# Graph network block: the first dense product starts per block of the counts' matrix; key comparison in loops from broadcast rows

## The chip, the cores and the metric

One core of a Trainium2 chip runs the whole program. The metric is the time of one execution in microseconds (us), the median of three runs. The core has TensorE (PE, matrix products), VectorE (DVE), ScalarE (ACT), GpSimd (POOL) and SyncE (SP), which run side by side and meet at semaphores. DMA engines move data between the core's memory and the chip's.

## The reference, cut to what matters

Four graph layers follow one another over 6250 nodes with 128 features and 100,000 edges sorted by destination. The part that matters here is the first layer, whose aggregation is applied twice:

```python
N_NODES, N_EDGES, D, K, ALPHA = 6250, 100000, 128, 2, 0.5
dst = jnp.minimum((6250 * uniform(100000) ** 2.0).astype(int32), 99999)   # sorted: low nodes hold most edges
for _ in range(K):
    msg = norm[:, None] * x[src]
    agg = jax.ops.segment_sum(msg, dst, num_segments=n)
    x = (1.0 - ALPHA) * agg + ALPHA * h
```

The second layer (edge attention), the third (two mean aggregations) and the fourth (gated sums) use the same edges. The third applies the same unweighted aggregation twice more.

## The kernel before, in words

**The matrix of counts.** The four unweighted aggregations are done as dense products. A matrix of bf16 counts lies in the chip's memory (`d_adj`): 52 row blocks (`VBLOCKS`) of 128 rows, and 49 column blocks (`BLOCKS`) of 128 source nodes. Its rows are numbered in the order in which destination nodes first appear among the sorted edges, with one extra row at every boundary between pairs of tiles, so edges that come later write rows that lie later.

**How it is filled.** SP first fills it with zeros (`zero_sp`, L455, 52 transfers). The 782 tiles of 128 edges are then written by GpSimd (`scatter_pool`, L474): one indirect DMA for each tile, 128 elements of two bytes each, to the addresses in one column of `address`. At most 16 tiles are under way (`adj_out`). Tiles are grouped in 49 batches of 16 (`BATCH * U`).

**Equal edges.** Two edges of a pair of tiles with the same source and destination must not be written twice: one of them must write the total count and the other must be sent elsewhere. So every batch is compared before it is written. TensorE turns each tile's keys (`key_col`) into rows in PSUM (`same_pe`, L557); VectorE compares a pair's row of 256 keys with the column of one tile (`same_dve`, L569) and sums what is equal, which leaves a read of the accumulator behind every comparison; three short steps for each batch (L576 to L578) then correct the addresses. ScalarE copies the counts (`counts_act`, L590), once the zeros under them have landed, and that releases GpSimd for the batch. The comparison is straight code for 784 tiles. Nothing makes VectorE wait for the writes, so it may run any number of batches ahead of GpSimd.

**Order around it.** GpSimd writes 12 batches (`FIRST_BATCHES`), then gathers 49 tiles for the node ends (L1725) and 14 tiles for the step tables (L1731), then writes the other 37 batches. VectorE sets up keys (`pairs_dve`), compares 12 batches, makes the tile and step tables (L1842 to L1877), compares the other 37, and only then computes the statistics of x (L1013), the degrees (L1890), the places of row blocks against node blocks (`v_steps_dve`, with 100 straight comparisons at L673), the step rows and the derived weights. It then opens the product (`dense_open`). TensorE follows the same order.

**The product.** `dense_pe` multiplies every row block with the source rows in three bf16 pieces (L764, 49 matmuls of 384 columns for each of 52 row blocks), while `dense_sp` loads half blocks four deep (L717). Before the first load SP waits in `scattered` until all 782 writes have landed. The product is done four times; the second follows the first at once.

Of the kernel before, what the change touches and what calls it, by code (L numbers as in the profile page):

```python
# [6 lines left out]
P = 128  # L7
# [3 lines left out]
BLOCKS = -(-NODES // P)  # L11
# [26 lines left out]
assert BATCHES * BATCH == TILE_PARTS  # L38
LATER = 512.0
# [6 lines left out]
FIRST_BATCHES = 12  # L46
# [85 lines left out]
def program(nc, a, out):  # L132
# [6 lines left out]
    with ExitStack() as ctx:  # L139
# [24 lines left out]
        tab_gate = scratch("tab_gate", (BLOCKS * P, GATE_ROW))  # L164
        d_steps = [scratch(f"d_steps{k}", (STEP_PAD,), I32) for k in range(2)]
# [30 lines left out]
        v_row, b_row, first_row = (step_rows[V_ROW:V_ROW + 1, k * P:k * P + VSTEPS] for k in range(3))  # L196

# [80 lines left out]
        weigh = part(acc_flat, weigh_at, (2, 2, P))  # L278
        other = part(acc_flat, weigh_at + 4 * P, (COLS,), I32)
        is_later = part(acc_flat, weigh_at + 4 * P + COLS, (2, BATCH * U), I32)  # L280
        place_col = part(t_flat, 0, (COLS,), I32)
        same = part(hot_flat, 0, (2, U, PAIR), BF16)
        count_f = part(hot_flat, U * PAIR, (TILE_PAD,))
# [85 lines left out]
        class Sums:  # L369
# [30 lines left out]
            def step_pe(self, pe, message, arrived):  # L400
                def step(i, r):
# [3 lines left out]
                    pe.sem_inc(sem("pe_turn"), 1)  # L405
# [36 lines left out]
        ASKED = "pairs_counted pair_tops pairs_ready keys_ready node_rows node_ends v_counts v_starts v_cols".split()  # L442
        ANSWERED = "pairs_summed pair_cols node_rows_summed v_summed v_starts_wide v_cols_wide".split()
# [4 lines left out]

        zero_in = [sem(f"zero_in{k}") for k in range(2)]
# [15 lines left out]
        def scatter_pool(pool, first, last):  # L465

            for n in range(first * BATCH, last * BATCH):
# [3 lines left out]
                if n >= PARTS:  # L471
                    pool.wait_ge(adj_out[r], 16 * U * (n // PARTS))
                for tile in range(n * U, min((n + 1) * U, TILES)):
                    pool.indirect_dma_start(d_adj, bass.IndirectOffsetOnAxis(address[:, tile:tile + 1], 0),  # L474
                                            counts[:, tile:tile + 1], None).then_inc(adj_out[r], 16)

        def scattered(engine):
            for r in range(PARTS):
                tiles = sum(1 for tile in range(TILES) if tile // U % PARTS == r)
                engine.wait_ge(adj_out[r], 16 * tiles)  # L480

        def pairs_dve(dve, chain):

            nc.vector.memset(ones, 1.0)
            chain.after(nc.vector.tensor_tensor(tri, iota[:], step_no[:, 0:1].broadcast_to((P, P)), ALU.is_ge))
            nc.vector.memset(weigh[:, 0, 1, :], 1.0)
            nc.vector.memset(weigh[:, 1, 0, :], 1.0 + LATER)
            chain.after(nc.vector.tensor_scalar(weigh[:, 0, 0, :], tri, -LATER, 1.0 + LATER, ALU.mult, ALU.add))
            chain.after(nc.vector.tensor_copy(weigh[:, 1, 1, :], weigh[:, 0, 0, :]))
# [16 lines left out]
            chain.after(nc.vector.tensor_copy(pair_dst, pair_v))  # L506
# [1552 lines left out]
```

## Time and profile before

| what | us |
|---|---|
| median of three runs (7149.84 to 7160.71) | 7150.75 |
| the profiled execution's own time | 7143.62 |
| its span, first to last instruction | 7141.8 |
| first to last write of counts | 49.6 to 1258 |
| first matmul of the first product | 1390.7 |

The granted TensorE clock is 0.50 of full speed while the counts are written, 0.97 in the first product, and 0.737 as a mean. Times of day below are us from the start of the span. Busy time of an engine is the time in which its instructions execute; what released an idle engine is inferred from semaphores, and "remote" means that the profile found no engine for it. The rows themselves stand further below, in numbered groups.

### The profile page before, as it was taken

Reading aid. Unit: us, or ns where it says so; the run is one execution under the profiler, and the core shown is the slowest. Engines: PE = TensorE matmul, PEld = TensorE weight load, DVE = VectorE, ACT = ScalarE, POOL = GpSimd, SP = SyncE. Lnnn points to the kernel's source line nnn. Section 1 sums busy time; section 2 is a strip of 40 time slices with the busy share of each in tenths; the row PEclk is TensorE's granted clock in tenths of the full one; section 3 lists DMA queues with packets and bytes.
Section 4 is the critical chain, followed back from the end, with each engine's and each line's share of the span. In section 5 each row is a group of like instructions: output and inputs, shape, how many; then the busy total and the mean of one; then the engine's idle time right before and its main releaser. Section 6 shows DMA issues by size and latency. Waiting matters only on the chain.

```text
span 7141.8 us, 95188 instructions
## 1 busy us (share of the span) xinstructions
PE 4253.1 (60%) x24721; PEld 3361.3 (47%) x24722; DVE 3016.1 (42%) x9093; ACT 1323.9 (19%) x3278; POOL 2801.1 (39%) x2784
## 2 busy tenths in 40 slices
PE   2111211299899555565554565699799666666664
PEld 1101111166566444555554464466566656555664
DVE  4323333611311444444445777311411555555556
ACT  0000000200000211111111564300200323232223
POOL 5666666000000155565554464100000155555555
PEclk5555555599999777777777897899999755656556
DMA  9500000166465355555553351365365222222222
GB/s 341 176 15 0 0 0 0 40 197 197 136 197 171 75 151 155 153 161 159 159 154 116 97 149 54 108 195 164 107 195 166 58 78 78 79 79 79 79 78 69
DMA packets 440419, 833.75 MB, mean 117 GB/s; under 512 B 90922, under 2 KB 277260, under 8 KB 440190
## 3 DMA queue, kind: packets, MB, share of 16 engines
q1 hardware_dynamic: 333406, 608.36, 26.9%
q0 software_dynamic: 106912, 224.30, 12.0%
q8 instruction: 33, 0.54, 0.0%
q14 instruction: 68, 0.56, 0.0%
HBM read 677.55 MB, written 154.83 MB: 117 GB/s over the span
## 4 chain that ended last, share of the span: by engine, by line
PE 31%; DVE 24%; issue 20%; another core or an unknown queue 17%; DVEq 4%; ACT 2%; DMA 1%; SPq 1%; ACTq 0%; POOL 0%; POOLq 0%
PE ps L764 23%; DVE work L569 5%; DVE work L1531 3%; PE ps L920 2%; DVE work L360 2%; PE ps L407 2%; DVE work L1130 1%; DVEq L334 1%; DVE hw L430 1%; PE ps L771 1%; DVE t L430 1%; DVE acc L430 1%; DMA work<-attr_dram 1%; PE ps L1112 1%
## 5 line engine op out<-in xcount | busy, mean ns | idle before, releaser
L353 POOL DMA_INDIRECT work<-tab_kv,src_col x832 | 818.5, 984 | 1791.0 <-DMA tab_kv<-hw 1181.7
L353 POOL DMA_INDIRECT work<-tab_gate,src_col x832 | 795.1, 956 | 1791.2 <-DMA tab_gate<-logits 1182.2
L474 POOL DMA_INDIRECT d_adj<-logits,address x782 | 758.6, 970 | 404.8 <-issue 233.9
L764 PE MATMUL ps<-hw 128*128 128x384 bf16 x5096 | 861.9, 330 | 51.5 <-DVE hw L743 37.9
L764 PE MATMUL ps<-hw,work 128*128 128x384 bf16 x5096 | 845.1, 326 | 0.0
L557 PE MATMUL ps<-ident,acc 128*128 128x128 f32 x784 | 216.9, 434 | 911.6 <-remote 650.8
L407 PE MATMUL ps<-work 128*128 128x136 f32 (+1 forms) x3328 | 651.1, 359 | 129.3 <-DVE acc L430 85.4
L764 PEld LDWEIGHTS ps<-hw 128*128 128x128 bf16 x5096 | 501.7, 99 | 382.9 <-issue 53.5
L407 PEld LDWEIGHTS ps<-work 128*128 128x128 f32 x3328 | 596.3, 264 | 162.7 <-issue 162.6
L803 DVE TENSOR_TENSOR work<-work,ps 128x128 f32 (+1 forms) x208 | 59.9, 288 | 1407.8 <-ACT work L795 1407.1
L764 PEld LDWEIGHTS ps<-hw,work 128*128 128x128 bf16 x5096 | 498.8, 98 | 317.7
L557 PEld LDWEIGHTS ps<-ident,acc 128*128 128x128 f32 x784 | 141.1, 218 | 987.1 <-remote 682.0
L1096 PE MATMUL ps<-ident,work 128*128 128x128 f32 x832 | 176.9, 350 | 651.7 <-ACT work L1086 247.4
L360 DVE TENSOR_TENSOR work<-iota,rels 128x512 f32<-128x512 f32 x520 | 357.1, 687 | 334.2 <-remote 295.1
L1493 PE MATMUL ps<-logits,work 128*128 x1664 | 340.0, 328 | 258.1 <-ACT work L1461 251.8
L1493 PEld LDWEIGHTS ps<-logits,work 128*128 128x128 f32 x1664 | 339.9, 302 | 295.7 <-issue 295.6
L569 DVE SCALAR_TENSOR_TENSOR work<-ps,acc 128x256 bf16<-128x256 f32 x784 | 342.6, 480 | 286.4 <-issue 285.0
L1127 DVE TENSOR_TENSOR work<-ps,work 128x512 f32<-128x512 f32 x208 | 143.2, 688 | 738.1 <-remote 521.8
L1096 PEld LDWEIGHTS ps<-ident,work 128*128 128x128 f32 x832 | 120.6, 178 | 684.9 <-issue 355.0
L1482 PE MATMUL ps<-ident,work 128*128 128x128 f32 x832 | 219.8, 416 | 279.7 <-DVE work L360 229.3
L795 ACT ACTIVATE work<-ps 128x128 f32 x208 | 57.6, 277 | 1631.9 <-PE ps L764 1631.9
L1085 ACT ACTIVATE work<-ps 128x512 f32<-128x512 f32 x208 | 124.2, 597 | 1221.7 <-remote 788.7
(377 smaller groups left out, 6492.7 us busy)
## 6 DMA issues: line engine op xcount, KB each, us to landing
hw<-d_adj SPq DMA_DIRECT2D x104, 800.0 KB, 4.3
work<-d_adj SPq DMA_DIRECT2D x104, 800.0 KB, 4.4
d_adj<-acc SPq DMA_DIRECT2D x52, 1568.0 KB
hw<-d_adj SPq DMA_DIRECT2D x104, 768.0 KB, 4.2
work<-d_adj SPq DMA_DIRECT2D x104, 768.0 KB, 4.3
work<-attr_dram SPq DMA_DIRECT2D x832, 64.0 KB
d_value<-work SPq DMA_DIRECT2D x208, 256.0 KB
work<-d_value SPq DMA_DIRECT2D x208, 256.0 KB, 2.7
```

The source lines that it names most:

```text
L353: pool.indirect_dma_start(rows[:, r * U + u, 0:width], None, table, bass.IndirectOffsetOnAxis(sources[:, at:at + 1], 0)).then_inc(rows_in[ ...
L360: nc.vector.tensor_tensor(hot[:, r * U:(r + 1) * U, :], iota[:].unsqueeze(1).broadcast_to((P, U, P)), rel_col[:, ds((i * PARTS + r) * U, U ...
L407: nc.tensor.matmul(self.place(r, u), hot[:, r * U + u, :], message(r, u), start=True, stop=True).then_inc(sem("win_done"), 1)
L430: nc.vector.tensor_tensor(nodes, nodes, self.place(r + u // U, u % U), ALU.add).then_inc(sem("win_added"), 1)
L474: pool.indirect_dma_start(d_adj, bass.IndirectOffsetOnAxis(address[:, tile:tile + 1], 0), counts[:, tile:tile + 1], None).then_inc(adj_out ...
L557: ins = nc.tensor.transpose(banks(n % SAME_RING)[:, u * P:(u + 1) * P], bcast_col(key_col[:, n * U + u:n * U + u + 1]), ident[:])
L569: ins = nc.vector.scalar_tensor_tensor(same[:, n % 2, u, :], banks(n % SAME_RING)[:, u // 2 * PAIR:(u // 2 + 1) * PAIR], key_col[:, tile:t ...
L764: last = nc.tensor.matmul(at, adj_half[2 * s + hf][:, k, :], xs[:, b, :], start=b == 0, stop=b == BLOCKS - 1)
L1096: nc.tensor.transpose(banks(0)[:, u * D:(u + 1) * D], attr[:, r * U + u, :], ident[:])
L1482: last = nc.tensor.transpose(banks(0)[:, u * P:(u + 1) * P], hot[:, r * U + u, :], ident[:])
L1493: last = nc.tensor.matmul(banks(2 + r % RING2)[:, u * 4:u * 4 + 4], hot_t[:, r % RING2, u * P:(u + 1) * P], logits_dst[:, ds(blocks[u], 1) ...
L1531: last = nc.vector.scalar_tensor_tensor(msg_gate[:, m, 0:D], rows[:, r * U + u, 0:D], msg_gate[:, m, D:D + 1], scaled[:, u, :], ALU.mult, ...
```

## The change

1. **Product by block.** `scattered` is gone. GpSimd counts landed parts of four tiles in `parts_landed`, and SP waits, before it loads row block v for the first product, until as many parts have landed as that block needs. The need is computed from the first row number of every pair (`v_begun`, one more small product on TensorE) into `parts_row`, from which SP reads one register for each block.
2. **Comparison.** The key rows come no longer from TensorE. ScalarE writes the keys to memory (`d_keys`) and loads for each batch the rows of 8 pairs, broadcast to all partitions (1 MB, two buffers). VectorE compares without an accumulator, and TensorE sums what is equal by products with a column of ones, two for each tile. All but a few batches run in engine loops of two batches, which need registers for their addresses and waits. The corrections of batch m stand inside the comparison of batch m + 1. `FIRST_BATCHES` is 13.
3. **Set-up.** The small tile table moves ahead of the key set-up on VectorE and TensorE, and the 49 gathers move ahead of the first writes on GpSimd. The 100 comparisons of `v_steps_dve` become a loop of 25 turns. Several semaphores become one (`turn`), which has no waiter.

Cut to its core:

```diff
@@ the last writes
-        def scattered(engine):
+        def scatter_end(pool):
             for r in range(PARTS):
                 tiles = sum(1 for tile in range(TILES) if tile // U % PARTS == r)
-                engine.wait_ge(adj_out[r], 16 * tiles)
+                pool.wait_ge(adj_out[r], 16 * tiles)
+                pool.sem_inc(sem("parts_landed"), 1)
@@ scatter_pool
                 if n >= PARTS:
                     pool.wait_ge(adj_out[r], 16 * U * (n // PARTS))
+                    pool.sem_inc(sem("parts_landed"), 1)
@@ dense_sp
                 v, hf, slot = n // 2, n % 2, n % 4
+                if j == 0 and hf == 0:
+                    parts, = registers(SP, parts_row, v, 1, TILE_PARTS)
+                    sp.wait_ge(sem("parts_landed"), parts)
                 wait(sp, sem("adj_used"), j * HALVES + n - 3)
@@ same_pe
-                for u in range(U):
-                    ins = nc.tensor.transpose(banks(n % SAME_RING)[:, u * P:(u + 1) * P], bcast_col(key_col[:, n * U + u:n * U + u + 1]), ident[:])
-                ins.then_inc(sem("same_keys"), 1)
+            def batch(m, half):
+                if not isinstance(m, int) or m >= 2:
+                    pe.wait_ge(sem("counts_ready"), m - 1)
+                for k in range(BATCH_PAIRS):
+                    pe.wait_ge(sem("same_made"), m * BATCH_PAIRS + k + 1)
+                    for u in range(2):
+                        at = counted(half)[:, 2 * k + u:2 * k + u + 1]
+                        nc.tensor.matmul(at, same[:, k, 0, u * P:(u + 1) * P], ones_col, start=True, stop=False)
+                        ins = nc.tensor.matmul(at, same[:, k, 1, u * P:(u + 1) * P], ones_col, start=False, stop=True)
+                    ins.then_inc(sem("same_summed"), 1)
@@ same_dve
-                        ins = nc.vector.scalar_tensor_tensor(
-                            same[:, n % 2, u, :], banks(n % SAME_RING)[:, u // 2 * PAIR:(u // 2 + 1) * PAIR], key_col[:, tile:tile + 1],
-                            weigh[:, u % 2].rearrange("p a b -> p (a b)"), ALU.is_equal, ALU.mult, accum_out=count_f[:, tile:tile + 1])
+                dve.wait_ge(key_in[half], (m - half) * 8 + 16)
+                for k in range(BATCH_PAIRS):
+                    if not isinstance(m, int) or m >= 1:
+                        dve.wait_ge(sem("same_summed"), (m - 1) * BATCH_PAIRS + k + 1)
+                    for j in range(2):
+                        ins = nc.vector.scalar_tensor_tensor(same[:, k, j, :], key_rows[:, half, k, :], key_col[:, ds(m * BATCH_TILES + 2 * k + j, 1)],
+                                                             weigh[:, j, :], ALU.is_equal, ALU.mult)
+                    ins.then_inc(sem("same_made"), 1)
+                    if k == 1 and not begin:
+                        decode(m - 1, 1 - half)
@@ counts_act
+            def load(m, half):
+                act.dma_start(key_rows[:, half].rearrange("p q e -> p (q e)"),
+                              d_keys[ds(m * BATCH_PAIRS, BATCH_PAIRS), :].rearrange("q e -> (q e)").partition_broadcast(P)).then_inc(key_in[half], 16)
...
+            def batch(m, half, ahead=True, real=P):
                 act.wait_ge(sem("targets_ready"), m + 1)
+                if ahead:
+                    load(m + 2, half)
```

**VectorE in the comparison.** Before, one batch after another in straight code (L569 the comparison, L576 to L578 the corrections):

```order
L569 SCALAR_TENSOR_TENSOR work<-ps,acc 128x256 x16
L576 TENSOR_SCALAR acc<-work 128x16
L577 TENSOR_TENSOR acc<-acc 128x16
L578 TENSOR_TENSOR address<-address,acc 128x16
L569 SCALAR_TENSOR_TENSOR work<-ps,acc 128x256 x16
```

Now, the start of the loop's body (L624 the comparison, L610 to L615 the corrections; ISA and REGISTER_ALU rows set addresses and waits):

```order
L585 UNCONDITIONAL_BRANCH
L585 ISA
L622 REGISTER_ALU
L624 ISA
L624 SCALAR_TENSOR_TENSOR work<-hw,acc 128x256
L624 ISA
L624 SCALAR_TENSOR_TENSOR work<-hw,acc 128x256
L622 REGISTER_ALU
L624 ISA
L624 SCALAR_TENSOR_TENSOR work<-hw,acc 128x256
L624 ISA
L624 SCALAR_TENSOR_TENSOR work<-hw,acc 128x256
```

The comparison reads the loaded rows in `hw` instead of PSUM, and nearly every instruction has one more before it that sets its address. The body of two batches has 98 rows: 38 instructions that compute, 39 ISA and 21 that calculate or branch.

**GpSimd up to the last write.** Before (L474 writes counts, L1725 gathers for the node ends, then 14 gathers for the steps):

```order
L474 DMA d_adj<-logits,address 41846784x1 x192
L1725 DMA hw<-dst_tiles_dram,work 128x128 x49
L1731 DMA work<-dst_tiles_dram,step_i 128x128
L1731 DMA work<-src_tiles_dram,step_i 128x128
```

Now:

```order
L1795 DMA hw<-dst_tiles_dram,work 128x128 x49
L484 DMA d_adj<-logits,address 41846784x1 x208
L1802 DMA work<-dst_tiles_dram,step_i 128x128
L1802 DMA work<-src_tiles_dram,step_i 128x128
```

The 49 gathers come first and no longer stand between two parts of the writes.

**SP in the first product.** Now a register load from the needs stands ahead of every pair of loads; before, the pairs followed each other without it:

```order
L342 TENSOR_LOAD step_rows
L789 DMA hw<-d_adj 128x3200
L789 DMA hw<-d_adj 128x3072
L342 TENSOR_LOAD step_rows
L789 DMA work<-d_adj 128x3200
L789 DMA work<-d_adj 128x3072
```

## Rows read from the trace of the kernel before

**Rows 1.** Busy time by stretch: x counts instructions; then clock, DMA share, GB/s.

```profile
core 0: us, PE busy (x) PEld busy (x) DVE busy (x) ACT busy (x) POOL busy (x), PEclk, DMA share, GB/s
49.00:1258.00 1209.00, 211.09 (x768) 138.63 (x768) 401.42 (x1702) 72.37 (x99) 821.42 (x845) 0.50 0.21 65
1258.00:1391.00 133.00, 20.80 (x97) 16.88 (x98) 90.01 (x348) 31.27 (x69) 0.00 (x0) 0.53 0.06 20
1391.00:1850.00 459.00, 443.66 (x2702) 274.69 (x2701) 92.80 (x273) 22.95 (x61) 0.00 (x0) 0.97 0.57 184
```

**Rows 2.** Waits of GpSimd, 40 to 1260: total us, times, longest.

```profile
POOL d_adj L474 <- issue: 233.9, 766, 0.5
POOL d_adj L474 <- ACT logits L590: 166.0, 15, 44.2
```

**Rows 3.** Timeline of GpSimd: start, us, instruction, idle before it in brackets.

```profile
49.64 1.16 POOL L474 DMA_INDIRECT d_adj<-logits,address  x1 [44.16 <-ACT logits L590]
...
1096.05 0.97 POOL L474 DMA_INDIRECT d_adj<-logits,address  x1 [0.30 <-issue]
1106.91 0.97 POOL L474 DMA_INDIRECT d_adj<-logits,address  x1 [9.89 <-ACT logits L590]
1108.18 0.97 POOL L474 DMA_INDIRECT d_adj<-logits,address  x1 [0.30 <-issue]
...
1174.65 0.97 POOL L474 DMA_INDIRECT d_adj<-logits,address  x1 [7.04 <-ACT logits L590]
```

**Rows 4.** Timeline of VectorE, a batch from 1123 to 1171.

```profile
1122.97 0.17 DVE L578 TENSOR_TENSOR address<-address,acc 128x16 int32<-128x16 int32 x1
1123.42 0.48 DVE L569 SCALAR_TENSOR_TENSOR work<-ps,acc 128x256 bf16<-128x256 f32 x1 [0.28 <-issue]
1123.83 0.08 DVE L569 DVE_READ_ACCUMULATOR work<-ps,acc 128x1 f32 x1
...
1136.62 0.08 DVE L569 DVE_READ_ACCUMULATOR work<-ps,acc 128x1 f32 x1 [0.93 <-issue]
1138.01 0.48 DVE L569 SCALAR_TENSOR_TENSOR work<-ps,acc 128x256 bf16<-128x256 f32 x1 [1.31 <-issue]
1139.42 0.08 DVE L569 DVE_READ_ACCUMULATOR work<-ps,acc 128x1 f32 x1 [0.92 <-issue]
...
1168.17 0.17 DVE L576 TENSOR_SCALAR acc<-work 128x16 int32<-128x16 f32 x1 [9.73 <-remote]
1169.58 0.18 DVE L577 TENSOR_TENSOR acc<-acc 128x16 int32<-128x16 int32 x1 [1.24 <-DVE acc L576]
1170.97 0.18 DVE L578 TENSOR_TENSOR address<-address,acc 128x16 int32<-128x16 int32 x1 [1.21 <-DVE acc L577]
```

**Rows 5.** Busy time of all engines in 17, 48 and 15 us about it.

```profile
1106.00:1123.00 17.00, 8.23 (x30) 5.44 (x31) 12.51 (x64) 2.12 (x4) 12.44 (x13) 0.50 0.02 1
1123.00:1171.00 48.00, 5.16 (x20) 3.15 (x18) 9.13 (x36) 1.50 (x2) 33.94 (x36) 0.50 0.02 0
```

**Rows 6.** Timeline of VectorE: the loop over the statistics of x.

```profile
1239.23 1.79 DVE L1013 BATCH_NORM_STATS2 work<-x  x7 [0.19 <-issue]
1242.49 0.29 DVE L1013 BATCH_NORM_STATS2 work<-x  x1 [1.48 <-issue]
...
1252.91 0.29 DVE L1013 BATCH_NORM_STATS2 work<-x  x1 [2.51 <-issue]
1255.71 0.29 DVE L1013 BATCH_NORM_STATS2 work<-x  x1 [2.50 <-issue]
...
1269.75 1.75 DVE L1013 BATCH_NORM_STATS2 work<-x  x7 [0.23 <-issue]
```

**Rows 7.** Timeline, all engines, 307 to 326.

```profile
307.82 0.63 PE L1789 MATMUL ps<-work 128*128 128x49 f32 x2
...
317.18 0.97 POOL L474 DMA_INDIRECT d_adj<-logits,address  x1 [0.31 <-issue]
324.78 0.21 DVE L1862 COPY work<-ps 128x49 f32<-128x49 f32 x1 [12.76 <-remote]
```

**Rows 8.** DMA issues: count, KB each, median us to landing.

```profile
biases<-biases_dram SPq DMA_DIRECT2D x1, 896.0 KB, 7.7
```

**Rows 9.** Timeline of TensorE: one row block, and a one-column product.

```profile
1310.68 0.38 PE L681 MATMUL ps<-work 128*128 128x1 f32 x2 [1.55 <-DVE work L649]
...
1823.36 8.13 PE L764 MATMUL ps<-hw,work 128*128 128x384 bf16 x49
```

More of the change, by code:

```diff
@@ L540, in pairs_pe @@
                 nc.tensor.transpose(banks(7)[0:1, c * P:(c + 1) * P], pair_small[:, 4, c:c + 1], ident[:])
+            pe.wait_ge(sem("asked"), ASKED.index("blocks_begun") + 1)
+            for c in range(PAIR_CHUNKS):
+                last = nc.tensor.matmul(banks(6)[:, 8:8 + VBLOCKS], ones, v_begun[:, c, :], start=c == 0, stop=c == PAIR_CHUNKS - 1)
+            last.then_inc(sem("answered"), 1)
             pe.wait_ge(sem("asked"), ASKED.index("pairs_ready") + 1)
@@ L547, in pairs_pe @@
             pe.wait_ge(sem("asked"), ASKED.index("keys_ready") + 1)
-        SAME_RING = 3
-        def same_pe(pe, first, last):
-            for n in range(first * BATCH, last * BATCH):
-                if n >= SAME_RING:
-                    pe.wait_ge(sem("same_counted"), n - SAME_RING + 1)
-                for u in range(U):
-                    ins = nc.tensor.transpose(banks(n % SAME_RING)[:, u * P:(u + 1) * P], bcast_col(key_col[:, n * U + u:n * U + u + 1]), ident[:])
-                ins.then_inc(sem("same_keys"), 1)
@@ L580, in counts_act, with counted, batches @@
-        def counts_act(act):
+        def counted(half):
+            return banks(3 + half)[:, 0:BATCH_TILES]
+        def batches(engine, first, last, step):
+            begin = first + 1 if first else 3
+            for m in range(first, begin):
+                step(m, m % 2)
+            with engine.Fori(0, (last - begin) // 2) as i:
+                for s in range(2):
+                    step(i * 2 + (begin + s), (begin + s) % 2)
+            if (last - begin) % 2:
+                step(last - 1, (last - 1) % 2)
@@ new lines, in same_pe @@
+        def same_pe(pe, first, last):
+            def batch(m, half):
[8 more added lines that the diff above has]
+                    ins.then_inc(sem("same_summed"), 1)
+            batches(pe, first, last, batch)
@@ L596, in program @@
+            with act.Fori(0, (BATCHES - 3) // 2) as i:
+                for s in range(2):
+                    batch(i * 2 + s, s)
+            batch(BATCHES - 3, 0)
+            batch(BATCHES - 2, 1, False)
+            batch(BATCHES - 1, 0, False, EDGES - (TILES - 1) * P)
         rows_i = part(rows_flat, 8 * P, (2, BLOCKS), I32)
```

192 lines of the change are left out of this document (108 added, 84 removed).

## The prediction

> **What bounds the kernel now.** I read the busy time by stretch first [rows 1]. Up to 1258 us GpSimd writes counts: 845 indirect DMAs (782 writes, 63 gathers) with TensorE busy 211 of 1209 us. From 1258 to 1391 nobody writes and VectorE makes the tables. From 1391 the first product runs at a clock of 0.97 and is over near 1850. The change can therefore win in three places: the writes may end earlier, the tables (133 us) may be made under the writes, and the product (52 row blocks of 8.13 us plus gaps, 427 us [rows 9]) may run under them. The last two need VectorE to have finished its comparisons early, because its tables stand behind all 49 batches in its program, before and after.
>
> So the question is what sets VectorE's pace. GpSimd issues a write every 1.27 us (1108.18 less 1106.91, [rows 3]), 20.3 us for a batch of 16. Its waits, however, are for ScalarE's counts, 166.0 us in 15 places, 44 of them at the start [rows 2], and ScalarE waits for VectorE's corrections. VectorE is no faster than GpSimd although nothing holds it back: all 784 comparisons at the undisturbed pace of 0.41 us (1123.83 less 1123.42, [rows 4]) would be 321 us.
>
> The timeline shows two phases. Shortly after GpSimd stood still (9.89 us before 1106.91 [rows 3]) VectorE does 64 instructions in 17 us; in the next 48 us, while GpSimd writes without a pause, it does 36 [rows 5]. In that dragged phase a comparison and its accumulator read start 1.4 us apart each (1136.62, 1138.01, 1139.42), the first correction waits 9.73 us for a semaphore of VectorE's own, and the two next corrections, 0.17 us of work each, start 1.4 us apart [rows 4]. TensorE's semaphores are late too: its tile sums end near 308.4, GpSimd's last write before its pause starts at 317.18, and VectorE sees the sums at 324.78 [rows 7]. I read this as a queue of completion events for each engine that drains one event in about 0.7 us while writes stream: two events for an instruction that computes, and 9.73 us for some 14 that are queued.
>
> **Is it the supply of code?** The loop over the statistics of x decides this for me [rows 6]. Its body is short and repeats. The first turn took 1.79 us for 7 instructions, the second turn, of the same code, 2.7 to 2.8 us for one (1255.71 less 1252.91), and once the writes were over a turn took 1.75 us again. Code that has just run is not missing. The Trainium skill ("Runtime: NRT & Kernel Launch", Instruction fetch mechanics) says the same from the other side: code is streamed in blocks, which is mostly hidden, and it is a taken branch out of the resident window that stalls, so that it prefers unrolled code. By that page the loops have no gain in supply at all; if the page were wrong for this case, the first rival below would be the outcome.
>
> **Part by part.**
> - *Comparison, dragged phase.* Before, a batch has 16 comparisons, 16 accumulator reads and 3 corrections: 35 at 1.4 us, 49 us; measured, from correction to correction, 48.0 us (1170.97 less 1122.97 [rows 4]). After, it has 19 instructions that compute, 26.6 us, and some 30 that set addresses, waits and branches. In the statistics loop each computing instruction has two such before it and a spacing of 2.8 us at most, 2.6 as a mean, which leaves 0.6 us for one [rows 6]. So 26.6 + 30 x 0.6 = 45 us. The bounds are 27 us (they cost nothing) and 48 us (0.7 each). I take 45, from the only row that has such instructions. It remains above GpSimd's 20.3 us, so VectorE again can't get ahead while writes stream.
> - *Comparison, free phase.* Before 7 us a batch: 16 x 0.41 and 0.6 for corrections. After, VectorE alone needs much the same, but each batch waits for a 1 MB load that is asked for one batch ahead; the nearest row is 896 KB in 7.7 us [rows 8]. TensorE adds 32 one-column products at 0.19 us (0.38 for two, [rows 9]), 6.1 us. I take 9 us; bounds 7 and 12.
> - *What that makes of the writes.* In a cycle of three batches GpSimd writes 61 us. VectorE has its free phase for the pause d and some 11 us after it, and the dragged phase for the other 50. Before, (11 + d)/7 + 50/48 = 3 gives d = 2.7 us; after, (11 + d)/9 + 50/45 = 3 gives 6.0. Sixteen cycles at 3.3 us more are 53 us. The trace's own pauses are longer than the 2.7 us that this balance gives for before (7.04 and 9.89 us in [rows 3]), so it is rough, and longer pauses give more quick time back; I take half, +27 us, with 0 and 53 as bounds.
> - *Gathers first.* The 49 gathers (62 us) now run from about 12 to 74 us, while VectorE makes its keys. Before, the first write stood at 49.64 [rows 3] and the gathers came later: together 112 us without waits. After, the keys' chain of small steps, with TensorE's answers, is exposed to the dragged phase and may be complete only when the gathers end; then 8 us of steps, a key load of 8, a batch of 9 and 3 for its corrections: first write at about 102. This is -10 us; bounds -35 (chain untouched, first write at 77) and +10.
> - *Tables between the batches.* VectorE's tile tables used to lie beside GpSimd's 49 gathers; now only beside 14. I expect a pause of some 20 us instead of 8: +12 us, bounds 0 and +30.
> - *Moves at no cost.* The writes themselves are unchanged; the wait for each part is the wait that was there. The loop in place of 100 straight comparisons adds registers to 25 turns, +5 us on the path. SP's register loads lie behind half blocks loaded four deep, and 8.2 us a block hides them; if that cover went, 52 x 0.5 us = 26 us. The 49 MB of key loads delay zeros whose need is far off.
> - *Product by block.* If VectorE is done with batch 49 about 20 us before the last write, as now, all parts have landed before the product opens. The waits then cost nothing, and give nothing.
>
> The sum against the profiled execution: 7143.6 + 27 - 10 + 12 + 5 = 7178 us; the runs' median is 7 us above that execution, so 7185. Between bounds: 7110 to 7240. I state 7180.
>
> **Rivals.**
> 1. *Comparison gets ahead.* If loops run at their quick pace under the writes, 49 batches of 9 us and 50 us of tables end near 590, the 133 us of set-up with some lag near 770, and the product needs 427 us more at full clock: 1200 instead of 1850, which is 6500 (6400 to 6700). For it: the whole stretch from 1258 on would lie under the writes. Against it: the loop in [rows 6]. The same rows also warn of TensorE, whose 98 loads and matmuls for each block might crawl. Chance 0.16.
> 2. *Only computing instructions count.* With 27 us in the dragged phase GpSimd is hardly ever starved: its 845 DMAs at 1.27 us and a start at 95 end near 1150 instead of 1258, so about 7040 (6990 to 7100). For it: the 16 accumulator reads of each batch are gone. Chance 0.19.
> 3. *TensorE's events bound the batch.* It has 64 loads and products for a batch instead of 32. If each costs two events of 0.7 us, that is 90 us in the dragged phase, and its 56 instructions before the late semaphore of [rows 7] fit that. Two batches to a cycle then need (11 + d)/9 + 30/90 = 2, d = 4, as against 2.7 in three: 49 batches give +54 us, with the other terms 7230 (7190 to 7290). Chance 0.22; from 20.3 us a batch upward every 1 us that is not caught up costs 49.
> 4. *The change doesn't do what it says:* the first product opens after the last write and no block waits. This is what I forecast in any case except rival 1.
>
> **How the numbers follow.** Forecast 0.38, rivals 1 to 3 0.16, 0.19 and 0.22, anything else 0.05. The point is the forecast's. The range leaves out rival 1 and a little on top: 6990 to 7290. About 0.2%, 14 us, can be told from no change here. Faster by more: 0.16 + 0.19 + 0.06 of the forecast's lower end, 0.41. Same: 0.11. Slower: 0.48.
>
> **What would show it.** In the profile after: the dragged phase between batches with one computing instruction in 1.4 us and the others in 0.6; pauses of GpSimd for ScalarE's counts as long as before or longer; last write between 1230 and 1310; first matmul of the product some 130 us behind it, at its full pace from the first block. I am wrong if the last comparison ends hundreds of us before the last write, or if loops show no dragged phase; then the first product begins before 1000 us and the loads wait on landed parts.

## The result and the profile after

| | before | after |
|---|---|---|
| median of 20 runs each, us | 7150.22 | 7128.10 |
| lowest to highest, us | 7126.52 to 7168.02 | 7082.84 to 7161.20 |
| profiled execution, us (span) | 7143.6 (7141.8) | 7082.84 (7080.9) |
| last count write starts, us | 1257.02 | 1227.41 |
| first matmul of the first product, us | 1390.70 | 1320.00 |

The changed kernel takes 0.9969 of the time before, 95% interval [0.9954, 0.9984]: 22 us less. The forecast was 30 us more, with 0.41 for "faster". The profiled execution is the quickest of the changed kernel's runs, so a trace difference of 60 us must not be read as the gain; three traces of nearly the same program below (changed, allwait, straight) spread over 51 us.

Busy time of all engines in four stretches of the changed kernel (columns as in [rows 1]):

```profile
100.00:150.00 50.00, 2.26 (x32) 1.47 (x32) 7.66 (x19) 1.47 (x2) 36.85 (x37) 0.50 1.01 345
350.00:450.00 100.00, 4.13 (x60) 2.76 (x60) 12.93 (x32) 1.47 (x2) 76.40 (x78) 0.50 0.12 31
500.00:700.00 200.00, 54.70 (x824) 37.93 (x824) 178.23 (x487) 21.28 (x38) 160.72 (x129) 0.50 0.39 136
750.00:1200.00 450.00, 17.54 (x63) 11.84 (x63) 42.60 (x146) 31.56 (x64) 344.57 (x339) 0.50 0.02 0
```

Between 350 and 450 us it is the dragged phase that the forecast expected: 78 GpSimd instructions in 100 us, one every 1.28 us, and 32 of VectorE's. Between 500 and 700 us it isn't: VectorE is busy for 178 of 200 us, batch after batch, and GpSimd makes only 129 writes, one every 1.55 us. The last run of comparisons (12 in a row) starts at 716 us, 511 us ahead of the last write. And then, from 750 on, the set-up of the first product crawls: 146 instructions of VectorE and 63 matmuls in 450 us, where the kernel before made 348 and 97 in 133 us without writes [rows 1]. This is the first half of rival 1 (the comparisons get ahead) without its gain.

Much of the dragged phase is not VectorE's own pace. Before it corrects a batch (L610) it waits for `same_summed`, TensorE's sums of that batch, here 26.8 and 53.2 us. TensorE's last product ahead of the first of these starts at 362.55 us, so the signal comes late, not the product:

```profile
389.19 0.17 DVE L610 SCALAR_TENSOR_TENSOR acc<-ps,acc 128x16 int32<-128x16 f32 x1 [26.80 <-remote]
467.17 0.17 DVE L610 SCALAR_TENSOR_TENSOR acc<-ps,acc 128x16 int32<-128x16 f32 x1 [53.19 <-remote]
```

Where the crawl lies, on ScalarE, in the loop over the rows of the first norm (timeline: start, us, instruction, idle before it):

```profile
807.80 2.42 ACT L1107 ACTIVATE t<-x,stat  x6 [2.14 <-issue]
...
860.28 0.49 ACT L1107 ACTIVATE t<-x,stat  x1 [5.11 <-issue]
863.09 0.49 ACT L1107 ACTIVATE t<-x,stat  x1 [2.31 <-issue]
865.89 0.49 ACT L1107 ACTIVATE t<-x,stat  x1 [2.31 <-issue]
...
882.68 0.49 ACT L1107 ACTIVATE t<-x,stat  x1 [5.11 <-issue]
...
947.08 0.24 ACT L1070 ACTIVATE stat<-stat 128x49 f32<-128x49 f32 x1 [2.30 <-issue]
```

Six activations at full pace (0.40 us each), then most of them 2.80 us apart; the 49 take 137 us. The trace has two register instructions for each: 2.80 = 1.40 + 2 x 0.70. With [rows 4] (a comparison and its accumulator read 1.40 us apart) and [rows 6] (2.8 us in a loop) one sum fits all of these: **0.70 us for a slot, two slots for an instruction that computes, one for any other.** VectorE's loop over the steps shows it again up to the last write, and soon after no longer:

```profile
1202.65 0.35 DVE L743 TENSOR_SCALAR_CACHE_REDUCE work<-hw,work 128x129 bf16 x1 [9.42 <-issue]
...
1220.88 0.35 DVE L743 TENSOR_SCALAR_CACHE_REDUCE work<-hw,work 128x129 bf16 x1 [9.44 <-issue]
...
1268.54 0.35 DVE L743 TENSOR_SCALAR_CACHE_REDUCE work<-hw,work 128x129 bf16 x1 [1.04 <-issue]
...
1270.86 0.35 DVE L743 TENSOR_SCALAR_CACHE_REDUCE work<-hw,work 128x129 bf16 x1 [1.04 <-issue]
```

A turn of four takes 18.2 us (1220.88 less 1202.65) under the writes and 2.3 us behind them, a factor of 8. The crawl outlives the writes: the last one starts at 1227.41, and the turn that starts at 1237.78 still takes 15.4 us.

GpSimd's group of all 782 writes, in the kernel before and in the changed one (busy us, mean ns; idle time ahead of them by what ended it):

```profile
L474 POOL DMA_INDIRECT d_adj<-logits,address x782 | 758.6, 970 | 404.8 <-issue 233.9 <-ACT logits L590 166.0 <-ACT logits L594 4.9
```

```profile
L484 POOL DMA_INDIRECT d_adj<-logits,address x782 | 848.1, 1085 | 276.6 <-issue 238.8 <-ACT logits L654 35.6 <-DMA d_adj<-logits,address 2.1
```

The waits for ScalarE's counts fall from 166.0 us [rows 2] to 35.6, but a write takes 1085 ns in place of 970, 90 us in all. The comparisons now read key rows from SBUF, where they read PSUM before, and it is beside them that writes are long. Counted in the changed kernel's trace, the 215 writes that lie beside them (VectorE busy for over 30% of the write) and beside no key load in flight take 1274 ns in the mean, and the 478 beside a VectorE that does little take 999. In the kernel before, 301 writes beside comparisons from PSUM take 967. That cost has no term in my sum, which took the writes as unchanged.

### The profile page after: what moved, and what is told of

Read it like the earlier page. It is cut to its first block, busy times and chain, and to the rows that moved or that the text cites. A ratio compares the mean times of both kernels' runs of the same rounds, so it can differ in the third digit from the quotient of the medians.

```text
span 7080.9 us, 98147 instructions
## 1 busy us (share of the span) xinstructions
PE 4162.5 (59%) x25513; PEld 3308.9 (47%) x25514; DVE 2977.6 (42%) x8318; ACT 1295.5 (18%) x3253; POOL 2894.8 (41%) x2784
## 4 chain that ended last, share of the span: by engine, by line
PE 33%; DVE 20%; issue 19%; another core or an unknown queue 15%; DVEq 6%; DMA 2%; ACT 2%; ACTq 1%; SPq 0%; POOL 0%; POOLq 0%
PE ps L836 23%; DVE work L1603 3%; PE ps L992 2%; DVE work L624 2%; PE ps L415 1%; DVE work L368 1%; DMA hw<-d_keys 1%; DVE work L1202 1%; DVEq L342 1%; PE ps L1184 1%; DVE hw L438 1%; PE ps L843 1%; PE ps L1182 1%; DMA work<-attr_dram 1%
## 5 line engine op out<-in xcount | busy, mean ns | idle before, releaser
L484 POOL DMA_INDIRECT d_adj<-logits,address x782 | 848.1, 1085 | 276.6 <-issue 238.8
L600 PE MATMUL ps<-acc,work 128*128 128x1 bf16 x784 | 93.8, 175 | 581.0 <-DVE work L624 308.3
L624 DVE SCALAR_TENSOR_TENSOR work<-hw,acc 128x256 bf16<-128x256 f32 x784 | 320.5, 479 | 114.6 <-DMA hw<-d_keys 52.5
L600 PEld LDWEIGHTS ps<-acc,work 128*128 128x128 bf16 x784 | 61.8, 104 | 613.6 <-issue 316.8
```

Of the source, the lines that this page charges most:

```text
L600: nc.tensor.matmul(at, same[:, k, 0, u * P:(u + 1) * P], ones_col, start=True, stop=False)
L624: ins = nc.vector.scalar_tensor_tensor(same[:, k, j, :], key_rows[:, half, k, :], key_col[:, ds(m * BATCH_TILES + 2 * k + j, 1)], weigh[:, ...
```

## Experiments

Each is the changed kernel (or the kernel before, where it says so) with one edit. All of them, where they wait on a register's value, mask it first, one register operation. The ratios are to executions of the kernel before taken beside each kernel's own, whose medians lie between 7143 and 7154 us. "Last compare" is the start of the last unbroken run of comparisons; "last write" and "product" are starts too, all from one trace of each kernel. In all 17 traces the rest of the program, from the end of the first product on, takes 5290 to 5323 us, so the time follows that end.

| kernel | us, median | ratio to before, 95% | last compare | last write | product |
|---|---|---|---|---|---|
| before | 7150 | 1 | 1226 | 1257 | 1391 |
| changed | 7128 | 0.9969 [0.9954, 0.9984] | 716 | 1227 | 1320 |
| allwait | 7141 | 0.9974 [0.9952, 0.9996] | 1190 | 1260 | 1392 |
| gathers_first (on before) | 7119 | 0.9970 [0.9960, 0.9981] | 1203 | 1237 | 1365 |
| gathers_late | 7185 | 1.0052 [1.0032, 1.0073] | 1092 | 1290 | 1419 |
| straight | 7107 | 0.9945 [0.9929, 0.9961] | 857 | 1234 | 1318 |
| hold30 | 7205 | 1.0082 [1.0053, 1.0110] | 917 | 1477 | 1071 |
| half | 7189 | 1.0067 [1.0047, 1.0087] | 1239 | 1291 | 1441 |
| thin128, a write every 1.36 us | 7030 | 0.9815 [0.9782, 0.9847] | 905 | 1304 | 1243 |
| thin192, 1.41 | 6934 | 0.9694 [0.9670, 0.9717] | 676 | 1320 | 880 |
| thin256, 1.47 | 6682 | 0.9351 [0.9336, 0.9367] | 573 | 1332 | 729 |
| thin320, 1.52 | 6752 | 0.9447 [0.9430, 0.9464] | 586 | 1377 | 743 |
| thin384, 1.58 | 6787 | 0.9499 [0.9483, 0.9515] | 562 | 1432 | 719 |
| mixed | 6707 | 0.9386 [0.9369, 0.9402] | 595 | 1347 | 750 |
| bunched256 | 6773 | 0.9485 [0.9456, 0.9514] | 584 | 1358 | 785 |
| allwait_thin256 | 7109 | 0.9948 [0.9933, 0.9964] | 582 | 1347 | 1367 |
| before_thin256 (on before) | 7086 | 0.9915 [0.9892, 0.9938] | 598 | 1323 | 1343 |

### Which part of the change gives the 22 us

**allwait.** The block-wise start taken back:

```
             sp.wait_ge(sem("dense_open"), j + 1)
+            if j == 0:
+                sp.wait_ge(sem("parts_landed"), TILE_PARTS)
```

> The changed kernel with the block-wise start taken back: SyncE waits for all parts of the counts before it loads the first half block. Both theories expect no difference (7080 to 7130 us), since the last write went out at 1227 us and the first matmul of the product at about 1310. If the block-wise start gives something, this one is slower by it.

0.9974 against 0.9969: no difference that the intervals can tell. In neither trace does the product open before the last write.

**gathers_first.** The kernel before, with the move alone (GpSimd's part; VectorE's and TensorE's tile counts and SyncE's load move with it):

```
-            scatter_pool(pool, 0, FIRST_BATCHES)
             pool.wait_ge(sem("next_tile"), 1)
...
+            scatter_pool(pool, 0, FIRST_BATCHES)
             pool.wait_ge(sem("step_tables"), 1)
```

> The kernel before with one part of the change alone: the 49 gathers, the tile counts on VectorE and TensorE and SyncE's load for them come first, the comparisons (still written out, with transposes) after them. My forecast's term for the move is -10 us (-35 to +10) and for the tables between batches +12 (0 to +30): -10 to +20 against before, 7140 to 7170 us. If the 22 us that the whole change gives come from the move, it reads 7120 to 7135; if from the comparison loops, 7145 to 7160.

0.9970: the move alone gives 21 us (0.30% of 7150), as much as the whole change. In its trace the first write starts at 78.1 us and GpSimd's waits for counts are 26 us shorter than before (GpSimd, 0 to 1310: total us, times, longest):

```profile
POOL d_adj L474 <- ACT logits L589: 140.0, 17, 12.9
```

**gathers_late.** The changed kernel with that same piece of the diff undone.

> The changed kernel without the move of the 49 gathers (and of the tile counts and SyncE's load that go with them): they lie behind the first 13 batches again; comparison loops, keys by DMA and the block-wise start stay. If the move is all that the change gives, this one reads as before: ratio 0.998 to 1.003, 7130 to 7165 us. If the loops give the gain of the whole and the move adds nothing to them, 0.996 to 0.998. If the loops cost time as my forecast's +27 us has it, 1.003 to 1.006.

1.0052: 37 us slower than before. So the comparison loops with their keys by DMA cost time where the gathers lie late, and the move is worth 59 us to them (1.0052 less 0.9969, of 7150). Its waits for counts (GpSimd, 0 to 1310: total us, times, longest) and its group of writes (0 to 1300: busy us, mean ns; idle time ahead of them):

```profile
POOL d_adj L484 <- ACT logits L654: 144.5, 7, 52.3
```

```profile
L484 POOL DMA_INDIRECT d_adj<-logits,address x782 | 820.9, 1050 | 384.8 <-issue 237.0 <-ACT logits L654 144.5 <-DMA d_adj<-logits,address 3.4
```

The waits are 166.0 us in 15 in the kernel before [rows 2] and 35.6 in 3 in the changed one. So even here the waits are 21.5 us shorter than before; the loss is in the writes themselves, 62 us longer than the 758.6 us of before. The parts don't add up: +37 for the loops and -21 for the move would be +16, and -22 was measured. What the loops cost depends on whether VectorE gets ahead, and the traces of the changed kernel, of straight and of allwait, which up to the last comparison are nearly one program, have their last comparisons at 716, 857 and 1190 us. One execution each can't say how often it does; the time is less sensitive to it (7083 to 7161 us over 20 runs), and in all three traces the product opens only behind the last write.

### What the crawl is

**straight.** The first norm's loops written out (VectorE's in the same way):

```
-            norm_act(act, 0, x, t, ACT.Relu, "h0_ready")
+            act.wait_ge(sem("norm_ready"), 1)
+            for g in range(GROUPS):
+                norm_rows(0, x, ACT.Relu, "h0_ready")(act, g, t)
```

> The changed kernel, with the loops over the statistics of x (VectorE) and over the rows of its norm (ScalarE) written out as 49 instructions each with fixed addresses. Two theories. S (supply): while GpSimd issues a count write every 1.27 us, each instruction, of any kind, reaches an engine only every 0.70 us, and a jump back throws away what was fetched ahead, so a loop pays 4 x 0.70 = 2.80 us a turn for an activation with its three address instructions. Q (events): 0.7 us for a completion event, two for a computing instruction. S expects 49 activations 0.70 us apart, 34 us in place of 139 (807.8 to 947.1 us), the statistics in 34 in place of 70, the first product some 80 to 140 us earlier, 6950 to 7010 us. Q expects 1.4 us apart, 69 us. If neither holds the spacing stays 2.8 us and the time 7080 to 7130.

Timeline of ScalarE in straight:

```profile
875.92 18.95 ACT L1107 ACTIVATE t<-x,stat 128x128 f32<-128x128 f32 x49 [2.09 <-DVE stat L1100]
894.78 0.23 ACT L1070 ACTIVATE stat<-stat 128x49 f32<-128x49 f32 x1
900.98 0.60 ACT L701 ACTIVATE hw<-ps 128x512 f32<-128x512 f32 x1 [5.97 <-PE ps L693]
...
913.41 0.60 ACT L701 ACTIVATE hw<-ps 128x512 f32<-128x512 f32 x1 [8.59 <-remote]
923.95 0.60 ACT L701 ACTIVATE hw<-ps 128x512 f32<-128x512 f32 x1 [9.94 <-remote]
```

Neither theory said this: all 49 at full pace, 0.39 us each, though writes go out every 1.27 us or more. From 904 us on, each copy of ScalarE's (L701) comes about 10 us after the one before, and it waits for TensorE's transposes (L693), four to a copy, both in straight code. So the crawl sets in with a delay, here some 40 us behind the last comparison (857 to 862), beside which writes had been long, and the 49 activations fell into that delay: this run doesn't decide between the theories for them.

Other rows do. Theory S gives every instruction of straight code 0.70 us. But in [rows 4] a comparison and its accumulator read, with no other instruction between them in the trace, are 1.40 us apart. (S counted three address instructions for an activation; the trace has two.) And the same straight code of the kernel before runs at full pace, a comparison and its read in 0.41 us, when only GpSimd's writes are thinned to one every 1.47 us (VectorE in before_thin256, further below):

```profile
597.62 0.47 DVE L573 SCALAR_TENSOR_TENSOR work<-ps,acc 128x256 bf16<-128x256 f32 x1
598.02 0.47 DVE L573 SCALAR_TENSOR_TENSOR work<-ps,acc 128x256 bf16<-128x256 f32 x1
```

So it is neither the loops' jumps nor the code's length. In the kernel with a 128x128 memset after each write (thin128) the loop of activations, not written out, also took 18.95 us:

```profile
928.51 18.95 ACT L1111 ACTIVATE t<-x,stat  x49 [2.19 <-DVE stat L1104]
```

In straight the set-up then crawled from 905 us on, so that the product opened at 1318: 0.9945 against the changed kernel's 0.9969, 17 us less, with intervals that overlap.

**half.** `address[0:64, ...]` and `counts[0:64, ...]` in each write; the other half of the counts is left out.

> The changed kernel, with each count write covering 64 of its 128 rows (the other rows' counts are left out). Theory W with one set of completions for a DMA, whatever its size: the others still get one slot in 0.70 us while writes go out every 1.27 us (if GpSimd issues faster, still less), time 7050 to 7150. Theory D: it is the 128 small elements of a DMA that take the channel; half of them leave the others at their full pace, the set-up is done near 900 us and the kernel takes 6650 to 6850 us.

A write every 1.20 us, and the crawl as before: 57 to 102 VectorE instructions in each 100 us from 100 to 1300 (a batch has 19), product at 1441, 7189 us against theory W's 7050 to 7150. So half the rows in a DMA don't help the others. But the edit halved less than it seems: in the traces a write moves 32 DMA packets in either kernel, 16 of 4 bytes and 16 of data (16 bytes each before, 8 now). Whether the others lose by the DMA, by its packets or by GpSimd's work of issuing it is not shown.

**hold30.** GpSimd stops ahead of batch 30 until the product is open:

```
+            scatter_pool(pool, FIRST_BATCHES, 30)
+            pool.wait_ge(sem("dense_open"), 1)
+            scatter_pool(pool, 30, BATCHES)
```

> The changed kernel, but GpSimd stops before batch 30 of the counts until VectorE has opened the first product, and writes the rest beside the product. S and Q: in the silence the set-up that took from 720 to 1310 us takes about 133 us, so the product opens near 870; then 19 batches of writes go out until about 1260. S further expects the product to crawl beside them, about 200 instructions a block at 0.70 us, 140 us a block, and to run at 8.2 us a block afterwards: end near 1670 in place of 1740, 7000 to 7030 us. If the product does not crawl beside writes it ends at 1300 to 1330 and the kernel at 6650 to 6700. If the set-up is slow for another reason than the writes, it ends as late as before and the writes later: 7150 to 7300.

The comparisons were not ahead in this run: the stop came at about 815 us, the last comparison at 917, and the writes ended at 1477. But the product, opened at 1071, shows the crawl on TensorE (timeline of its weight loads, of its matmuls):

```profile
1238.41 0.10 PEld L836 LDWEIGHTS ps<-hw 128*128 128x128 bf16 x1 [2.70 <-issue]
1241.21 0.10 PEld L836 LDWEIGHTS ps<-hw 128*128 128x128 bf16 x1 [2.70 <-issue]
```

```profile
1239.80 0.48 PE L836 MATMUL ps<-hw 128*128 128x384 bf16 x1 [2.33 <-issue]
1242.60 0.48 PE L836 MATMUL ps<-hw 128*128 128x384 bf16 x1 [2.32 <-issue]
```

A load and a matmul, 2.80 us, four slots: 137 us for a block of 49, against 8.13 [rows 9]. An early product under full-pace writes is worth next to nothing. My expectation of 140 us a block was right (its 200 instructions at 0.70 us are 98 at 1.40 in the trace); the 7000 to 7030 us fell with the late stop.

### Thinning the writes

**thin128, thin192, thin256, thin320, thin384.** A rest on GpSimd after each write:

```
                                             counts[:, tile:tile + 1], None).then_inc(adj_out[r], 16)
+                    pool.wait_ge(sem("rested"), tile)
+                    pool.memset(idle[:], 0.0).then_inc(sem("rested"), 1)
```

> The changed kernel with a 128x128 memset on GpSimd (0.2 us in this trace) after each of the 782 writes, so that none follows the one before within 1.27 us. If the slow supply needs writes at their full pace (as the stretch from 500 to 700 us suggests, where GpSimd's writes were themselves slowed and VectorE ran at its full pace), the set-up takes about 133 us from 720 or 850 on, the product runs beside the writes and ends shortly after the last one, near 1400 to 1450: 6740 to 6800 us. If the mere presence of writes slows the others, the last write only comes 156 us later: 7200 to 7260.

> The changed kernel with a memset of 128x256 on GpSimd after each write (an estimate of 0.34 us from the 0.22 us that the 128x128 memset took, so a write every 1.49 us in place of 1.37). Theory W: all engines' instructions and the completions of the writes pass through one channel of limited rate with a buffer; at a write every 1.27 us each other engine gets a slot per 0.70 us (measured), at 1.37 us one per about 0.37 us (a turn of VectorE's step loop took 9.6 us in place of 18.1), which in the writes' rate is linear: at 1.49 us one per 0.25 us. Then the set-up takes 150 to 180 us, but a load and matmul of the product still take 1.0 us in place of 0.17, and the last write comes 60 to 90 us later than with the shorter memset: 7040 to 7130 us. Theory T (threshold): above some spacing the others run undisturbed, the product too: 6750 to 6850 us.

> The same with a memset of 128x384 (an estimate of 0.45 us, a write every 1.6 us). W: a slot per 0.2 us, a load and matmul of the product in 0.8 us beside writes, last write near 1450 to 1480: 7130 to 7220 us. T: the product runs at 8.2 us a block beside the writes and ends just behind the last one: 6800 to 6880 us.

> The changed kernel with a memset of 128x192 on GpSimd after each write (an estimate of 0.28 us, so a write every 1.42 us; with 128x128 it was 1.37 us and 7030 us, with 128x256 1.47 us and 6682 us). If the others run well from a spacing just over 1.37 us on, the last write comes 40 to 50 us earlier than with 128x256 and the product ends as much earlier: 6630 to 6660 us. If what is left to the others grows in proportion to the time that is left between writes, the product beside them runs at half the pace of 128x256: 6750 to 6850 us.

> The changed kernel with a memset of 128x320 after each write (an estimate of 0.38 us, a write every 1.53 us; 1.47 us gave 6682 us, 1.58 us gave 6787). The last write comes about 40 us later than with 128x256. If the product beside the writes is then held by landed parts alone, it ends some 20 us behind the last write: 6700 to 6740 us. If it is still held by the writes' rate, as at 1.47 us, it ends 60 to 70 us behind: 6740 to 6780.

With 0.2 us more between writes the kernel is 6.5% faster than before. Windows of thin256 (first two rows) and of thin384, 900 to 1000 us:

```profile
600.00:700.00 100.00, 12.94 (x63) 9.63 (x63) 56.81 (x263) 23.00 (x56) 88.67 (x129) 0.53 0.02 0
900.00:1000.00 100.00, 79.52 (x413) 37.63 (x412) 8.25 (x32) 2.22 (x8) 88.02 (x137) 1.00 0.44 131
```

```profile
900.00:1000.00 100.00, 51.08 (x252) 28.23 (x251) 5.13 (x20) 1.39 (x5) 89.39 (x128) 0.75 0.24 81
```

In thin256 VectorE makes 263 set-up instructions in 100 us, where the changed kernel had 146 in 450; the product opens 156 us after the last comparison (573 to 729), near the 133 us without writes [rows 1]; and 413 matmuls in 100 us, at a clock of 1.00, run beside the writes, where hold30 had one in 2.80 us. The theory W as I had put it, linear in the writes' rate, missed by 360 us here: from 1.36 to 1.47 us per write the product's opening falls from 1243 to 729. The pace of the product beside the writes changes as steeply, but not in one jump. Its matmuls in 100 us are 33 to 36 in hold30 (1170 to 1470, a write every 1.27 us), 104 to 125 in thin192 (1000 to 1300, 1.41 us) and 326 to 395 in thin256 (900 to 1300, 1.47 us). Thin128 and thin192 missed both of their expectations: 7030 us lies between the two ranges, 6934 above both. The granted clock follows: 0.53 to 0.55 in thin192 there, and a matmul of 384 columns takes 0.48 us, where a single one takes 0.32 at a clock of 1.00 (thin256, below). From 1.47 us on the pace of the product depends on two things. In thin256 TensorE still has short gaps, and makes 413 matmuls (395 of them the product's) where full pace (49 in 8.13 us [rows 9]) is 603:

```profile
905.33 0.32 PE L840 MATMUL ps<-hw 128*128 128x384 bf16 x1 [0.38 <-issue]
906.07 0.33 PE L840 MATMUL ps<-hw 128*128 128x384 bf16 x1 [0.41 <-issue]
906.78 2.71 PE L840 MATMUL ps<-hw 128*128 128x384 bf16 x11 [0.39 <-issue]
```

In thin384 a block runs through once it begins, and waits for its parts before:

```profile
1015.62 9.45 PE L840 MATMUL ps<-hw,work 128*128 128x384 bf16 x49 [8.48 <-DMA work<-d_adj]
...
1034.13 10.43 PE L840 MATMUL ps<-hw 128*128 128x384 bf16 x49 [8.84 <-DMA hw<-d_adj]
```

```profile
SPq L793 <- POOLq L483: 362.9, 23, 24.0
```

(the second view: SyncE's queue, 900 to 1300, waits for GpSimd's landed parts for 363 of 400 us). From 1.47 us on each further 0.05 us only moves the last write, 45 to 55 us, and the time by 35 to 70.

**mixed.** `idle[:, 0:256 if tile < 420 else 320]`.

> The same with 128x256 after the first 420 writes and 128x320 after the others, which run beside the product. The last write comes about 20 us later than with 128x256 throughout. If the product then keeps up with the landed parts it ends some 20 us behind the last write, 6650 to 6680 us; if not, 6690 to 6720.

6707 us, between thin256 and thin320: no gain from longer rests beside the product.

**bunched256.** The rests in a row behind each batch of 16 writes:

```
+                if n % BATCH == BATCH - 1:
+                    for k in range(8):
+                        pool.wait_ge(sem("rested"), n // BATCH * 8 + k)
+                        pool.memset(idle[:], 0.0).then_inc(sem("rested"), 1)
```

> The changed kernel with the rest of GpSimd bunched: no memset after the single writes, but 8 memsets of 128x256 in a row behind every 16 writes, about the same 3.2 us for a batch as the 16 gaps of 0.2 us in the kernel with 128x256 after each write. If a buffer fills while writes go out every 1.27 us and only the mean rate of the writes counts, it behaves as that one: 6650 to 6750 us. If it is the spacing from one write to the next that slows the others, they crawl for 17 of every 20 us: 7000 to 7150 us.

6773 us, product at 785: 91 us above thin256 and 23 above the range I had expected, but far from 7000. With 16 writes in a row at 1.28 us the others crawl far less, if a pause follows. I read this as a buffer that takes up a burst, so that what counts is mostly the mean rate. It fits the delay in straight, the crawl that outlives the writes in the changed kernel, and [rows 5]: after 10 us without writes VectorE had 64 instructions at full pace before it was dragged again.

**allwait_thin256 and before_thin256.** The rests without the block-wise start, and on the kernel before:

> The changed kernel with a 128x256 memset after each write, and the block-wise start of the product taken back (SyncE waits for all parts). The product opens after the last write, 1332 us in the trace with the block-wise start, and takes 427 us: it ends near 1765 in place of about 1400, so 7040 to 7070 us against 6682. If the block-wise start is worth nothing here either, 6680.

> The kernel before, with a 128x256 memset on GpSimd after each write. It waits for all parts, so the product opens behind the last write as in the changed kernel without the block-wise start: 7040 to 7070 us. If its written-out comparisons of two instructions each still crawl beside writes every 1.47 us, the last write and the set-up come later: 7150 to 7300 us.

7109 and 7086 us, where I had expected 7040 to 7070 for both. In both the set-up is done by 800 us and TensorE then stands still until the last write, 1347 and 1323 (a window of allwait_thin256):

```profile
900.00:1000.00 100.00, 0.00 (x0) 0.00 (x0) 0.00 (x0) 0.00 (x0) 88.02 (x136) 0.50 0.02 0
```

So beside thinned writes the block-wise start is worth 427 us (7109 less 6682), where alone it gave nothing; and the loops and the move with it, 7109 against 7086, are 23 us worse than the kernel before's own code.

## Why the prediction was wrong

Two terms of the sum failed, and with either one put right the forecast would have been "same": the loops (27 + 5 us, measured about 0 beside the early gathers) and the move with the tables (+2 us, measured -21).

- **Dragged phase.** The cost of an instruction was right: 1.4 us for a computing one; 0.7 us for others, which I had at 0.6. For a batch 26.6 + 30 x 0.7 = 48 us; in the dragged stretch (32 VectorE instructions in 100 us, 19 to a batch) it was 59, above my upper bound, because VectorE waited 26.8 and 53.2 us for TensorE's sums: rival 3's mechanism. That the phase must last as long as writes stream was wrong: the stretch from 500 to 700 us. Its writes came every 1.55 us, a spacing at which the thinned kernels' engines hardly crawl, and they came so late because of VectorE's own comparisons beside them. So once quick, VectorE kept itself quick in this trace.
- **The loops** (writes cycle +27, step loop +5). The larger failed term. It held that writes stay as they are and that VectorE, never ahead, makes GpSimd's pauses longer. In the changed kernel's trace the pauses fell from 166.0 to 35.6 us and the writes grew by 90 us. Beside the early gathers the two come out even: 0.9969 with the loops, 0.9970 without. Gathers_late, which has the loops without the move, is 37 us slower than before. That is my term's size and sign by luck: its pauses fell too, by 21.5 us, and its writes grew by 62. Why the loops cost nothing beside early gathers and 37 us beside late ones stays open; there is one trace of each.
- **Gathers first and the tables** (-10 and +12). The other failed term. The first write starts at 85.9 us, not 102, and at 78.1 with the move alone, beside my bound of 77: the keys' chain hardly crawled beside the gathers. And no pause of 20 us came for the tables: GpSimd's last step gather is issued at 406.2 us in the kernel before and at 384.8 with the move alone, and it waits for nothing but the instruction ahead of it. The two terms came to +2, and measured -21 on the kernel before. With that in its place, the sum would have been 7178 - 23 = 7155 us, 7162 as a median; with the loops' 32 us at nothing as well, 7130, and 7128 was measured.
- **Product by block, 0.** Right (allwait), but not for my reason: the comparisons were done some 510 us ahead in this trace, and it was the crawling set-up that let the writes end first.
- **Rival 1** (6500 us) had this course, and its price left out the crawl of everything behind the comparisons. Thin256 shows the same kernel with the crawl gone: product from 729 us, 6682.
- **Rivals 2 and 3.** Neither sum is right as it stands. Of rival 2's 845 DMAs 49 lie before its start at 95, so it ends near 95 + 796 x 1.27 = 1106, not 1150; rival 3's terms give 7143.6 + 54 - 10 + 12 + 5 + 7 = 7212, not 7230. Neither enters the forecast.
- **Supply of code.** The dismissal was right; before_thin256, where the straight comparisons of [rows 4] run at full pace beside thinner writes, bears it out.
- **What would show it.** Last write 1230 to 1310 and first matmul some 130 us behind: 1227.4 and 93 us. "Wrong if the last comparison ends hundreds of us before the last write": so it did. That the product would then begin before 1000 us did not follow.

**What stays open** is what the slots are. The writes and the instructions of all engines seem to share something with a buffer and a limited rate; that is read from its effect only. It is no plain limit on instructions or on DMA packets: counted in the traces, thin256 starts 12.2 instructions and 44.8 packets in a us between 900 and 1000, and the changed kernel, crawling, 2.3 and 24.0 between 750 and 1200. The Trainium skill ("NOTIFIC — the notification-queue block", sections "The implicit engine gate", "Overflow: three behaviours, one of which stalls the engine" and "Constraints, capacities, measured rates") offers a candidate: in a full profile each instruction leaves a record at its start and its end, one block writes them, holds some 500, and its internal queues hold back an engine rather than lose one. Two slots for an instruction that computes would agree, one for a register instruction would not without more; and the 12.2 instructions in a us of thin256 speak against records of instructions alone. No run here was made without the profiler, so whether part of the crawl belongs to the measurement is not shown.

## What to carry to other kernels

Where one engine issues small DMAs back to back, look at whether all the others slow down to one spacing in the same stretch, loops and straight code alike; if so, work moved under those DMAs is hardly hidden, and a rest of 0.2 us after each may be worth more than any reordering (here 7128 to 6682 us). Try the enabling edit and the one that hides work together: block-wise start and rests gave nothing or under 1% alone and 6.5% together. And when a forecast rests on "this phase lasts while X streams", ask whether the edit itself changes X's pace.

## What the hardware showed that I had not expected

- The crawl fades steeply in the writes' mean spacing between 1.36 us (product opens at 1243 us), 1.41 us (880) and 1.47 us (729), and it sets in late: 49 activations ran at full pace in 18.95 us beside writes before it did, and bursts of 16 writes at 1.28 us with pauses behind them cost 91 us against evenly spread rests (6773 and 6682 us).
- A write of 64 rows moves as many DMA packets as one of 128, 32, and the others crawl beside it too: a write every 1.20 us, 7189 us.
- GpSimd's writes are longer beside VectorE's comparisons from SBUF: 1274 ns in the mean against 999 elsewhere in the same trace, 1085 over all 782 (970 before), single ones to 5.24 us. Beside comparisons from PSUM they are not (967).
